# A two-layer gated block with two mixtures of experts: first expert stage in 71 blocks of 128 rows, rows gathered by token, and both attentions reordered

## The reference

```python
x = x + tanh(g_xattn[0]) * cross_attention_0(layernorm(x), ctx)   # one head of 256
x = x + tanh(g_ffn[0])   * experts_0(layernorm(x))                # each token to 2 of 8 experts, 512 hidden
x = x + tanh(g_xattn[1]) * cross_attention_1(layernorm(x), ctx)   # 16 heads of 64, then Wo and bo
x = x + tanh(g_ffn[1])   * experts_1(layernorm(x))                # each expert takes its 256 best tokens per batch, 1024 hidden
```

## Time and profile before

| | |
|---|---|
| Time, median of 3 runs (lowest, highest) | 1656.74 us (1656.09, 1662.45) |
| The profiled execution | 1658.5 us; its span from first to last instruction 1656.8 us |
| PE busy | 1322.2 us, 80% of the span |
| DVE busy | 1078.2 us, 65% |
| ACT busy | 636.8 us, 38% |
| POOL busy | 574.5 us, 35% |
| Mean granted TensorE clock | 0.88 of full speed |
| DMA | 112.64 MB, mean 68 GB/s |

### The profile page before, as it was taken

How to read it: one execution, slowest core, us unless ns; L and a number is a source line. 1 busy time by engine, 2 the same in 40 slices (tenths; PEclk the granted TensorE clock), 3 DMA queues, 4 the chain that set the end, 5 groups by cost and what they waited for, 6 DMA issues and landing times. The chain is left out here.

```text
span 1656.8 us, 32133 instructions
## 1 busy us (share of the span) xinstructions
PE 1322.2 (80%) x10396; PEld 962.0 (58%) x10397; DVE 1078.2 (65%) x2382; ACT 636.8 (38%) x1901; POOL 574.5 (35%) x584
## 2 busy tenths in 40 slices
PE   5654426999999999788888885009999999999995
PEld 2543315889999947566666664003566566556554
DVE  2868663555555557799999997966655664665551
ACT  1433311432222236576767774203333332332321
POOL 1355570000000040587777772212223322422312
PEclk8555557999999978799999998558999999999998
DMA  5132322421121110011111112003233323322212
GB/s 184 54 127 70 122 96 81 126 89 64 62 64 63 64 33 1 27 52 51 51 41 47 51 44 99 10 20 146 64 102 69 85 68 97 79 73 65 33 19 26
DMA packets 63773, 112.64 MB, mean 68 GB/s; under 512 B 8145, under 2 KB 54098, under 8 KB 60626
## 3 DMA queue, kind: packets, MB, share of 16 engines
q1 hardware_dynamic: 45266, 78.10, 14.1%
q0 software_dynamic: 18432, 33.57, 9.3%
HBM read 73.89 MB, written 37.75 MB: 67 GB/s over the span
## 5 line engine op out<-in xcount | busy, mean ns | idle before, releaser
L1695 POOL DMA_INDIRECT out_x<-yo,gidx x64 | 101.4, 1584 | 338.9 <-ACT yo L1777 324.3
L1807 DVE SCALAR_TENSOR_TENSOR hid<-psU,sil 128x512 f32<-128x512 f32 x128 | 88.5, 691 | 196.6 <-ACT sil L1766 193.8
L1312 ACT ACTIVATE pr<-psS,mx 128x77 f32<-128x77 f32 x512 | 157.9, 339 | 35.7 <-DVE mx L1465 35.7
L1766 ACT ACTIVATE sil<-psG 128x512 f32<-128x512 f32 x128 | 76.4, 597 | 204.6 <-PE psU L112 193.5
L939 DVE SCALAR_TENSOR_TENSOR hid<-psU,sil 128x512 f32<-128x512 f32 x78 | 53.9, 691 | 134.7 <-ACT sil L905 134.7
L110 PE MATMUL psYb<-W1h,hh 128*128 128x256 f16 x512 | 139.6, 273 | 1.7 <-ACT yo L1777 1.7
L111 PE MATMUL psYb<-W1l,hh 128*128 128x256 f16 x512 | 139.6, 273 | 0.0
L112 PE MATMUL psYb<-W1h,hl 128*128 128x256 f16 x512 | 139.6, 273 | 0.0
L1025 POOL MEMSET K1h<- 64x2464 f16 x1 | 2.1, 2147 | 350.3 <-POOLq L820 350.3
L110 PE MATMUL psOL<-N,pt 128*128 (+1 forms) x320 | 88.3, 276 | 42.7 <-DVE lex L1493 41.9
L1312 ACT ACTIVATION_READ_ACCUMULATOR pr<-psS,mx 128x1 f32 x512 | 113.2, 221 | 0.0
(11 more groups left out here) (331 smaller groups left out, 4220.3 us busy)
## 6 DMA issues: line engine op xcount, KB each, us to landing
w1s<-in_w SPq DMA_DIRECT2D x16, 1536.0 KB, 6.4
stage<-in_w SPq DMA_DIRECT2D x8, 1536.0 KB
bx<-x_rows SPq DMA_DIRECT2D x39, 256.0 KB, 2.7
y_rows<-yo SPq DMA_DIRECT2D x39, 256.0 KB, 2.1
X<-in_x SPq DMA_DIRECT2D x8, 512.0 KB, 8.8
out_x<-X SPq DMA_DIRECT2D x32, 128.0 KB, 1.9
n_rows<-xs SPq DMA_DIRECT2D x32, 128.0 KB, 2.1
x_rows<-xa SPq DMA_DIRECT2D x9, 256.0 KB
```

The lines of the kernel that those rows point to most:

```text
L1312: ins = act.activation(pr1[:, par, h * LK:(h + 1) * LK], psS1[:, q, i * LK:(i + 1) * LK], ACT.Exp, bias=mx1[:, h:h + 1], scale=1.0 / (SX * ...
L1695: pool.indirect_dma_start(out_rows[:, :], bass.IndirectOffsetOnAxis(gidx[:, half, col:col + 1], 0), yo1[:, j % 2, n, :], None, compute_op= ...
L1766: act.activation(sil1[:, f % 2, :], psG1[f % 2][:], ACT.Silu, scale=1.0 / (SX * SW)).then_inc(d_sil, 1)
L1807: dve.scalar_tensor_tensor(hid1[:, f % 2, :], psU1[f % 2][:], SH / (SX * SW), sil1[:, f % 2, :], ALU.mult, ALU.mult).then_inc(d_hid, 1)
```

## The change

**Attention 0.** Setup and attention are one block of the program. The constants come in through two DMA queues, and PE starts after four of the transfers. The two normalisations move from DVE to ACT (with a small `shift` on DVE). The router takes fp32 rows and fp32 weights, 8 matmuls per group for 24, so the second split goes. The weights of the two experts are worked out per group. The scatter writes 8 bytes per token and expert, the token number and its weight, into a table `tab`, no longer the row; the normalised rows and `X` are stored once, in order, in `n0_rows` and `x1_rows`. The table is filled beforehand with numbers of dump rows, in place of the zeros behind each region. All orders and lags are new.

**Experts 0.** Blocks of 128 rows, 71 of them. SP loads the block's piece of the table; POOL gathers its rows by token from `n0_rows` and adds the results, already multiplied by the token's weight, by indirect DMA into `x1_rows`; each add waits until the one before has landed.

**Attention 1.** `X` is read back from `x1_rows` (8 DMAs) during the stage before; the gathers and both combines go. The bias comes in as one more row of `N1` (written by a DMA at the end of the stage before). The probabilities are transposed as fp32 (10 transposes) and split as they leave PSUM: three high parts on ACT, three low parts on DVE. The router's logits stay in PSUM for all tiles, fp32, and its softmax is done once at the end. New orders.

**Experts 1.** `n_rows` holds fp32; 8 fp32 transposes per block for 16 fp16, and the split happens on the way out of PSUM.

```diff
-BR = 256
+BR = 128
+NB = BR // P
 NB0 = (2 * B * S + E * (BR - 1)) // BR
...
-                            pool.indirect_dma_start(x_rows[:, :], bass.IndirectOffsetOnAxis(slots[:, par, c, k:k + 1], 0),
-                                                    xc[:, par, k, :], None, bounds_check=E * REG - 1,
+                            pool.indirect_dma_start(tab[:, :], bass.IndirectOffsetOnAxis(slots[:, par, c, k:k + 1], 0),
+                                                    tokw[:, GT * g + k, c, :], None, bounds_check=E * REG - 1,
...
+                def normalise(n):
...
+                            act.activation(dst, X[:, GT * g + i, :], ACT.Identity, bias=shift[n][:, par, i:i + 1],
+                                           scale=rstd[n][:, par, i:i + 1]).then_inc(s_xn[n], 1)
...
-                def load(j, par):
-                    wait(sp, b_xt, j - 1)
+                def load_table(j, par):
+                    if not isinstance(j, int) or j >= 2:
+                        sp.wait_ge(b_tab[par], 16 * (j // 2))
                     row = sp.value_load(blkrow[0:1, bass.ds(j, 1)], min_val=0, max_val=E * REG)
...
+                def gather(j, ph):
+                    par = j % 2
+                    pool.wait_ge(b_tab[par], 16 * (j // 2) + 16)
+                    wait(pool, b_xt, j - 1)
+                    for n in range(NB):
+                        pool.indirect_dma_start(bx[:, par, n, :], None, n0_rows[:, :],
+                                                bass.IndirectOffsetOnAxis(tabs[:, j, n, 0:1], 0)).then_inc(b_in[par], 16)
+
+                def add(j, ph):
+                    par = j % 2
+                    pool.wait_ge(b_yo, j + 1)
+                    wait(pool, b_out[1 - par], 16 * NB * ((j + 1) // 2))
+                    for n in range(NB):
+                        pool.indirect_dma_start(x1_rows[:, :], bass.IndirectOffsetOnAxis(tabs[:, j, n, 0:1], 0),
+                                                yo[:, par, n, :], None, compute_op=ALU.add).then_inc(b_out[par], 16)
+                pipeline(pool, NB0, BDEPTH, [(0, gather), (3, add)], straight=True)
...
-                    for n in range(2):
+                    for n in range(NB):
                         rows = slice(n * P, (n + 1) * P)
                         for f in range(FT):
                             at = bass.ds(w + (DOWN + f * D), D)
...
+                for g in range(NG):
+                    sp.dma_start(X[:, GT * g:GT * g + GT, :], x1v[:, GT * g:GT * g + GT, :]).then_inc(u_x, 16)
+                sp.wait_ge(u_b, 2)
+                sp.wait_ge(u_nl, 5 * B)
+                sp.dma_start(N1[HP * KR:HP * KR + 1, :, HP, :], bo4[:].rearrange("p b a d -> p b (a d)")).then_inc(u_x, 16)
...
-                            for part in range(2):
-                                ins = pe.transpose(psP1[n % 2][:, c - a_, part, :], ps1[:, par, part, c * P:(c + 1) * P], identh[:])
+                            ins = pe.transpose(psP1[n % 2][:, c - a_, :], pn1[:, par, c * P:(c + 1) * P], ident[:])
...
+                def probs_high(n):
+                    def run(t, par):
+                        a_, b_ = CH[n]
+                        act.wait_ge(c_pt[n], t + 1)
+                        wait(act, c_av[n], t)
+                        act.activation(pt1[:, a_:b_, 0, :], psP1[n % 2][:, 0:b_ - a_, :], ACT.Copy, scale=SP).then_inc(c_ph, 1)
+                    return run
...
+                def probs_low(n):
+                    def run(t, par):
+                        a_, b_ = CH[n]
+                        dve.wait_ge(c_ph, 3 * t + n + 1)
+                        dve.scalar_tensor_tensor(pt1[:, a_:b_, 1, :], psP1[n % 2][:, 0:b_ - a_, :], SP, pt1[:, a_:b_, 0, :],
+                                                 ALU.mult, ALU.subtract).then_inc(c_pe[n], 1)
+                    return run
...
-                def combine(c):
...
-                def copy_probs(n):
```

More of the change, by code:

```diff
@@ L244, in program @@
         xv = a["x"].rearrange("b (t p) d -> p (b t) d", p=P)
[L245 to L331, removed]
@@ L344, in program @@
         s_xh = [sem(f"s_xh{n}") for n in range(2)]
-        s_xl = [sem(f"s_xl{n}") for n in range(2)]
+        s_xl = sem("s_xl")
         s_sc = sem("s_sc")
@@ L433, in _ @@
             def _(act):
-                def high(n):
-                    def run(g, par):
-                        wait(act, s_lg if n else s_sc, g - 1)
-                        for k in range(KD):
-                            act.wait_ge(s_xt[n], KD * g + k + 1)
-                            act.activation(xth[n][:, par, k, :], psT[:, k, :], ACT.Copy, scale=SX).then_inc(s_xh[n], 1)
-                    return run
-                def weights_high(g, par):
+                act.dma_start(wqT, a["wqT0"].rearrange("(k p) d -> p k d", p=P)).then_inc(s_w2, 16)
@@ new lines, in high_in, with high_out @@
+                def high_in(g, par):
+                    wait(act, s_sc, g - 1)
+                    for k in range(KD):
+                        act.wait_ge(s_xt[0], KD * g + k + 1)
+                        act.activation(xth[:, par, k, :], psT[:, k, :], ACT.Copy, scale=SX).then_inc(s_xh[0], 1)
+                def high_out(g, par):
+                    wait(act, s_lg, g - 1)
+                    for k in range(KD):
+                        act.wait_ge(s_xt[1], KD * g + k + 1)
+                        act.activation(xto[:, par, k, :], psT[:, k, :], ACT.Copy).then_inc(s_xh[1], 1)
@@ L450, in exps, with gap_exp @@
                     act.activation(pr[:, par, :, :], pr[:, par, :, :], ACT.Exp, scale=1.0 / (SX * SM)).then_inc(s_exp, 1)
+                def gap_exp(g, par):
+                    act.wait_ge(s_gap, g + 1)
+                    wait(act, s_wt, 4 * (g - 1))
+                    act.activation(gape[:, par, :], gap[:, par, :], ACT.Exp).then_inc(s_gape, 1)
                 def probs_high(g, par):
@@ L1028, in _ @@
                     pool.memset(V1[i][0:DH, :, :, KM:P], 0.0).then_inc(u_z, 1)
-                for t in range(2):
-                    gather_y(pool, t)
             @block.tensor
@@ L1383, in run @@
                             wait(pe, c_res, t)
-                            wait(pe, c_ls, before(t, "outputs0", "logits", PE_ORDER, T))
                         for c in range(a_, b_):
@@ L1707, in transposes @@
                     for k in range(KD):
-                        for part in range(2):
-                            for n in range(NT):
-                                at = part * D + k * P
-                                last = pe.transpose(psXb[:, k, part, n * P:(n + 1) * P], gx[:, par, n, at:at + P], identh[:])
+                        for n in range(NT):
+                            last = pe.transpose(psXb[:, k, n * P:(n + 1) * P], gx[:, par, n, k * P:(k + 1) * P], ident[:])
                     last.then_inc(d_xt, 1)
```

582 lines of the change are left out of this document (316 added, 266 removed).

## The result

The changed kernel takes 1750.5 us (median of 4 runs, 1747.0 to 1752.0) beside 1659.4 for the one before (4 runs on the same chip, 1656.1 to 1662.5): a ratio of 1.055, 95% interval 1.052 to 1.058. The forecast was 1772, with 1690 to 1865 as its range.

A forecast was written before the change was run, and what follows sets the result against it. PE bounds both expert stages, DVE attention 1, a chain of waits attention 0; experts 0 was to become sequencer-bound. Profiled 1658.5 + 202 - 38 - 55 + 6 = 1773.5, so 1772 measured, range 1690 to 1865.

The forecast's parts named there:

- The 7.2 us per block: Experts 0: PE's sequencer sets each 128-row block at 7.2 us, 71 blocks; stage 543 us, +202.
- The rival of the array as the bound: Experts 0: the array stays the bound, stage 320 us (-21), kernel 1550; chance 0.10.
- the pace of the sustained rule: Experts 0: 81 ns per 128-column matmul, block 5.4 us, stage 405 (+64), kernel 1635; chance 0.06.
- the 10 us taken for it: Experts 0: 10 us added because the clock may be at its low level in some stretches.
- the 0.25 a triple: Experts 0: PE's sequencer works 0.25 us per triple of matmuls with register addresses, where the array needs 0.33 at 256 columns.
- A block of waiting adds: Experts 0: each POOL add waits for the one before, so a block cannot be under about 3.9 us.
- the first rival: Experts 0: the sequencer's 0.25 was back pressure and the array stays the bound; stage 320 us, kernel 1550; chance 0.10.
- PE busy about 60%: Experts 0: sign that the forecast is right, beside a stage of 500 to 560 us and results 7.2 us apart.
- the 17.5 put down to POOL: Attention 0: a group falls from 25.6 to about 20 us, 17.5 where POOL's issue sets it.
- the tile falls from 10.71 to 8.8, with 8.3 if PE's waits vanish: Attention 1: PE becomes the tallest engine; 9.8 if half the gain goes to new waits; stage -55 us (-75 to -30).
- The sum of DVE's removed work: Attention 1, per tile: two combines 2.67 us, three copies 1.76, low parts 1.48 and about 0.4, small router operations 0.8.
- The rest: Products +3 us, last add +2, experts 1 +1, together +6; reading `X` back hidden in the products.

## Why the prediction was right, and where it was off

**Experts 0, right.** The 7.2 us per block was read as the sum of the sequencer's own steps under an array that hid them, and the stage gives 7.21. The rival of the array as the bound is refuted by the block itself, and so is the pace of the sustained rule. The clock stayed up, so the 10 us taken for it were not there. Three blocks of about 10 us, while the pieces of the next stage's weights are split, cost 9, and that they stand where 10 had been taken for the clock is luck; the other blocks are 7.09 apart. The one weak point of the argument was that the 0.25 a triple had never been seen without an array in front of it. The trace of the changed kernel and the three kernels with fixed addresses settle it: 0.12 for each register instruction. One bound was read too low. A block of waiting adds was put at "about 3.9 us"; the chain of adds takes 4.57, above the array's 4.2, so the first rival's stage of 320 us was out of reach as well: with no register work at all the stage took 369. And "PE busy about 60%" reads 76% in the row of the stage, for the reason given there; by its starts the array is busy 4.2 of 7.2.

**Attention 0, right in size for a base that does not last.** The group was forecast at 20 us, from 25.6. With scatters it is 17.8 in the mean of three (a group's eight scatters begin at 112.8 and again, three groups on, at 166.4), and the single groups go from 19.3 down to 16.4, so the 17.5 put down to POOL is no floor. Five groups at 17.8 would have won 39 and not 27, but the whole stage won 35 for a forecast of 38, so the start and the end did not give the 11 taken for them; that the total fits is partly luck. And a good half of the gain is the wait of 7.3 us, which the same kernel does not have on another chip. The error was to take a wait whose releaser the profile calls only "remote" as one for PE's logits and as the kernel's own: the logits of the group that was read had ended 6.8 us before DVE started.

**Attention 1, the right direction by a term of the wrong size.** The term that was mis-sized reads "the tile falls from 10.71 to 8.8, with 8.3 if PE's waits vanish"; that PE becomes the tallest was right. I took PE's busy time of 8.85 as near its need. Its need is the distance of its matmuls' starts, read in the trace of the changed kernel: 30 x 0.109 for the outputs, 24 x 0.131 for the scores, 10 x 0.109 and 4 x 0.109 for the transposes, 4 x 0.112 for the logits, 8.39 us, and the tile is 8.34:

```profile
890.00:898.35 8.35, 8.35 (x74) 7.24 (x73) 7.56 (x16) 7.05 (x39) 3.93 (x6) 1.00 0.11 34
```

32 x (10.71 - 8.35) = 76, less the ends, are the 73 measured. (Before the change the tiles alternate between 10.7 and 11.0, so 10.71 was the shorter of two.) The sum of DVE's removed work was right as time and wrong as work: of a combine's 1.34 us, 1.12 remained with 8 columns, a wait behind POOL. A reader who planned to make the combines cheaper by that sum would have gained 17 us for 32 x 2.67 = 85.

For the same reason the forecast of DVE itself failed. It was to fall "to about 5, or 6.5", idle a quarter of the tile, and it is busy 7.45 of 8.34. With the combines gone another small operation stands where POOL multiplies, an operation of 128 x 8 elements that took 0.15 us in the kernel before (first row) and now takes 0.84 in the mean (second row):

```profile
L1465 DVE TENSOR_SCALAR mx<-mx 128x8 f32<-128x8 f32 x4 | 0.6, 148 | 0.0
...
L1482 DVE TENSOR_SCALAR mx<-mx 128x8 f32<-128x8 f32 x16 | 13.4, 840 | 0.3
...
901.37 1.92 POOL L1309 TENSOR_TENSOR pn<-pr,sum 128x1024 f32<-128x1024 f32 x1 [0.28 <-DVE sum L1488]
...
901.76 1.55 DVE L1482 TENSOR_SCALAR mx<-mx 128x8 f32<-128x8 f32 x1
```

Two a tile at 0.69 more each are 1.4 us, and without them DVE would be busy 6.1. It costs nothing here, since the array sets the tile.

**The rest.** Products +2.8 for +3, experts 1 +2.8 for +1, reading `X` back hidden as said (60 GB/s in the row of the products for 9 before).

## What to carry to other kernels

Where addresses come from a register, count the sequencer's instructions per block beside the array's matmuls. They don't shrink with the block, so halving a block can move the bound from the array to the sequencer at a stroke; look for it before, under PEldq, as a pace with little slack. Take a matmul's cost from the distance of two starts, not from its busy time, and before a long DVE operation is called work, look at what POOL did in the same microsecond. When the profile names who ended a wait and the start comes later than usual behind it, look for a second condition that was met at almost the same time.

Here the two good halves combine: blocks of 256 rows with everything else of the change run in 0.956 of the time before.

## What was not expected of the hardware

A `scalar_tensor_tensor` of 128 x 8 elements took 0.68 or 1.55 us, according to which POOL instruction stood beside it. It goes the other way too: in the earlier trace rows's tile POOL's scalar operation on 128 x 1 elements, usually 0.22 us, took as long as DVE's split of the probabilities beside it.

```profile
847.72 1.58 POOL L1242 TENSOR_SCALAR rs<-mv 128x1 f32<-128x1 f32 x1 [0.38 <-issue]
847.73 1.48 DVE L1449 SCALAR_TENSOR_TENSOR ps<-pn,ps 128x1280 f16<-128x1280 f32 x1
```

And the same program ran 1.6% faster on one chip than on another (1633 and 1659 us), nearly all of it in one stage and beside one wait that was not explained; the changed kernel differed by 0.1% (1748.1 and 1750.5).
